# A column range for each chunk of edges in the matrix build, 196 instead of 120 of the first network's sum products inside it, and its dense layers spaced evenly

## The reference, cut to what matters

```python
src = randint(100000, 0, 3125)
dst = sort(3125 * uniform(100000) ** 2)          # sorted, dense at low numbers
h = maximum(layernorm(x), 0)
aggr = segment_sum(h[src], dst)                  # network 0
z = (1 + eps) * h + aggr
z = relu(relu(z @ W1 + b1) @ W2 + b2)
x = x + log_softmax(z)
# networks 1 to 3: again sums over the edges, dense layers, norms
```

## Time and profile before

| | us |
|---|---|
| runs | 1205.87, 1209.30, 1209.38 |
| median | 1209.3 |
| the profiled execution: its time | 1203.78 |
| its span, first to last instruction | 1202.1 |
| setup ahead of the first half | 22.7 |
| the build, halves 0 to 55 | 22.7 to 272.7 |
| rest of network 0 up to D(6) | 272.7 to 353.4 |
| the three other networks | 353.4 to 1202.1 |

### The profile page before, as it was taken

The page is one execution under the profiler, slowest core; times in us unless marked ns, Lnnn a source line. Parts: engine busy times, 40 slices in busy tenths (PEclk is TensorE's granted clock), DMA queues, the critical chain, the costliest instruction groups (busy, mean ns, idle before and its releaser), DMA issues.

```text
span 1202.1 us, 19388 instructions
## 1 busy us (share of the span) xinstructions
PE 1119.6 (93%) x6353; PEld 659.0 (55%) x6353; DVE 671.5 (56%) x1984; ACT 444.5 (37%) x1330; POOL 10.9 (1%) x36
## 2 busy tenths in 40 slices
PE   3778899999989999999898998996899999999997
PEld 3556666665554554545545545544555556544544
DVE  7999899994562235456366455365644325632211
ACT  4669988886561122211300201102421214811100
POOL 1000000000000000000000000000000000000000
PEclk9997999999989999999999998998899999999998
DMA  2100000002001013433224142399932314500001
GB/s 74 28 2 1 2 2 10 2 2 50 6 11 26 15 39 81 93 78 78 48 60 90 30 91 56 76 254 193 206 87 69 89 35 107 130 25 26 17 21 31
DMA packets 208276, 70.32 MB, mean 58 GB/s; under 512 B 180949, under 2 KB 207284, under 8 KB 208174
## 3 DMA queue, kind: packets, MB, share of 16 engines
q1 hardware_dynamic: 124702, 42.31, 16.4%
q10 hardware_dynamic: 83152, 25.52, 9.6%
q0 software_dynamic: 320, 1.22, 0.5%
HBM read 20.71 MB, written 28.26 MB: 41 GB/s over the span
## 4 chain that ended last, share of the span: by engine, by line
PE 81%; DVE 8%; DMA 4%; issue 2%; ACT 2%; ACTq 1%; DVEq 1%; SPq 0%
PE PS L1223 51%; PE PS L928 9%; PE PS L2728 4%; PE PS L917 2%; PE PS L1600 2%; PE PS L2216 2%; DMA di_d<-SM 2%; PE PS L893 2%; DVE HPb L792 2%; PE PS L2179 2%; PE PS L1718 1%; DVE HPb L789 1%; DVE HPb L737 1%; ACT ADJ L964 1%; DMA s_d<-SM 1%
## 5 line engine op out<-in xcount | busy, mean ns | idle before, releaser
L1223 PE MATMUL PS<-ADJ,HPb 125*128 125x500 bf16 (+2 forms) x2250 | 443.6, 353 | 0.0
L1223 PEld LDWEIGHTS PS<-ADJ,HPb 125*128 125x128 f16 x2250 | 219.1, 98 | 215.6 <-issue 21.9
L964 ACT CAST ADJ<-PS 126x72 f32 (+7 forms) x784 | 193.2, 315 | 44.3 <-PE PS L928 15.1
L1223 PE MATMUL PS<-ADJ,Zf 125*128 125x500 bf16 (+2 forms) x1050 | 202.1, 352 | 0.0
L928 PE MATMUL PS<-HPb 128*128 128x150 bf16 (+3 forms) x784 | 192.2, 350 | 4.3 <-ACT ADJ L964 3.1
L1223 PEld LDWEIGHTS PS<-ADJ,Zf 125*128 125x128 f16 x1050 | 102.4, 98 | 93.8 <-issue 1.3
L917 PEld LDWEIGHTS PS<-HPb 128*128 128x128 bf16 x642 | 85.2, 143 | 55.3 <-issue 31.0
L1910 DVE CUSTOM_DVE_ANT_0 HPb<-ADJ,HPb 125x625 bf16<-125x625 bf16 x125 | 101.4, 811 | 6.4 <-DMA HPb<-di_d 1.5
L917 PE MATMUL PS<-HPb 128*128 128x25 bf16 x642 | 87.4, 213 | 8.6 <-DVE HPb L792 7.1
L928 PEld LDWEIGHTS PS<-HPb 128*128 128x128 bf16 x784 | 85.6, 159 | 7.9 <-ACT ADJ L964 6.2
L2050 DVE BATCH_NORM_STATS2 WB<-PS 128x6 f32<-128x500 f32 (+2 forms) x28 | 17.6, 630 | 123.1 <-PE PS L2179 123.1
(11 more groups left out here) (363 smaller groups left out, 1112.8 us busy)
## 6 DMA issues: line engine op xcount, KB each, us to landing
adj_d<-ADJ ACTq DMA_DIRECT2D x25, 700.0 KB
HPb<-y_d SPq DMA_DIRECT2D x19, 187.5 KB, 2.8
HPb<-di_d SPq DMA_DIRECT2D x10, 250.0 KB, 3.3
adj_d<-ADJ ACTq DMA_DIRECT2D x25, 81.2 KB
ADJ<-in_x SPq DMA_DIRECT2D x1, 1562.5 KB
q_d<-HPb SPq DMA_DIRECT2D x25, 62.5 KB
HPb<-di_d SPq DMA_DIRECT2D x5, 305.2 KB
HPb<-s_d ACTq DMA_DIRECT2D x5, 250.0 KB, 3.8
```

Of the source, the lines that this page charges most:

```text
L964: e.copy(to, WPS[group % BANKS][0:PD, t0 * RESTS[q]:t1 * RESTS[q]] .rearrange("p (t d) -> p t d", t=t1 - t0)).then_inc(s_mv, 1)
L1223: mm = e.matmul(accs[q], H[0:PN, t, q, 0:P], cols, start=(t == 0 and (two or q == 0)), stop=(t == NT - 1 and (two or q == 1)), skip_group_ ...
```

## The change

Six things change:

- **A column range for each chunk.** `KEYS[k][c]` gives, for quarter k and chunk c of the group, the range of target columns that it may touch. Chunk 0 takes 0 to `HEADS[k]`, chunk 1 takes from `FROM[k]`. New checks on the input send other data to the general build; the data of this case meets them.
- **The key's order.** It is now target first, tile second (`25 * target + tile`). One table of numbers, `TAB`, serves all ranges as a slice. ACT's copies read the bank with 100 bytes from target to target (before, contiguous), and PE's joined first column is written contiguously (before, with a stride).
- **DVE writes key one-hots for chunk c of two groups together**, in all quarters, by a two-operand compare of 350+350, 350+500, 500+750 and 600+850 elements for two groups. The ring has 3 slots of two groups each.
- **PE** makes the joined first column from chunk 0 alone, and its big products have 150+150, 150+250, 225+375 and 275+425 columns.
- **196 sum products in the build:** one behind every group in halves 28 to 55. These are the ranges 0 to 2 and 46 products of range 3. 154 are left behind it, of which 54 have 500 columns.
- **Dense steps evenly spaced:** behind the build, in slots of 2 products, range c = 0 to 4 has its steps at slots 7+15c, 11+15c and 15+15c (with D(c) in the last), and `turned_z(c+1)` at 9+15c. D(5) and D(6) stay where they are in network 1's first sums. The diagonal's first part is added later, ahead of `answered(3)`.

In the setup, POOL makes one table rather than several, DVE has 8 more short comparisons for the checks, and ACT copies the keys in another layout.

```diff
-RING = 7
+RING = 3
+HEADS = (6, 6, 9, 11)
+FROM = (1, 1, 2, 4)
...
-    EARLY0, EARLY_PER = 26, 4
+    EARLY0, EARLY_PER = 28, HG
...
+    KEYS = [((0, HEADS[k] + 1), (FROM[k] if k else 0, WINS[k])) for k in range(KR)]
+    KWS = [[(c1 - c0) * NT for c0, c1 in v] for v in KEYS]
...
-                for k in range(KR):
-                    line(e.scalar_tensor_tensor(out=t3[:, k, :], in0=k3[:, k, :], scalar=float(WINS[k]), in1=t3[:, k, :],
-                                                op0=ALU.mult, op1=ALU.add))
+                line(e.scalar_tensor_tensor(out=til_f, in0=til_f, scalar=float(NT), in1=key_f, op0=ALU.mult, op1=ALU.add))
...
+                for k in range(KR):
+                    line(e.tensor_scalar(w[1][:, k:k + 1], w[3][:, k:k + 1], float(FROM[k] - 1), None, ALU.is_le))
+                    line(e.tensor_scalar(flags[:, k, 7:8], w[3][:, k:k + 1], float(HEADS[k]), None, ALU.is_gt))
...
+                def one_hots(u, c):
+                    q, g = u * 2 // QG, u * 2 % QG
+                    k0, k1 = KEYS[q][c]
+                    e.tensor_tensor(key_pair(q, u, c), TAB[:, k0 * NT:k1 * NT, :],
+                                    KTH[q][:, c, g:g + 2].rearrange("p (o g) -> p o g", o=1)
+                                    .broadcast_to([P, KWS[q][c], 2]), ALU.is_equal).then_inc(s_oh, 1)
...
-                        if q >= PAIRED:
-                            e.tensor_scalar(key_hot(q, n0 + m), IOK[q], KT[:, n0 + m:n0 + m + 1], None, ALU.is_equal)\
-                             .then_inc(s_oh, 1)
...
+                        at = h * HC + m
+                        if at % 2 == 0:
+                            unit, c = n // 2 * HG + at // (2 * GC), at // 2 % GC
+                            if unit >= RING:
+                                e.wait_ge(s_ohx, (unit - RING + 1) * 2 * GC)
...
-                        for c in range(GC):
+                        for c in range(1 if joined else GC):
...
-                            e.matmul(WPS[group % BANKS][:, 0:rests * NT], OHP[h][:, :, g * GC + c],
-                                     key_hot(q, m)[:, NTP:KWS[q]], start=(c == 0), stop=(c == GC - 1),
+                            c0, c1 = max(KEYS[q][c][0], 1), KEYS[q][c][1]
+                            e.wait_ge(s_oh, keys_told(group // 2, c))
+                            e.matmul(WPS[group % BANKS][:, (c0 - 1) * NT:(c1 - 1) * NT], OHP[h][:, :, g * GC + c],
+                                     key_hot(q, group, c, c0, c1), start=(c == 0), stop=(c == GC - 1),
...
-                        if n >= EARLY0 and g % 2 == 0:
-                            early_sum((n - EARLY0) * EARLY_PER + g // 2)
+                        if n >= EARLY0:
+                            early_sum((n - EARLY0) * EARLY_PER + g)
...
-                            e.copy(to, WPS[group % BANKS][0:PD, t0 * RESTS[q]:t1 * RESTS[q]]
-                                   .rearrange("p (t d) -> p t d", t=t1 - t0)).then_inc(s_mv, 1)
+                            e.copy(to, WPS[group % BANKS][0:PD, 0:RESTS[q] * NT]
+                                   .rearrange("p (d t) -> p t d", t=NT)[:, t0:t1, :]).then_inc(s_mv, 1)
...
-                    if c + 1 == WHOLE and not general:
+                    if c + 1 == PLAIN and not general:
                         first_diagonal()
...
-                LAG = 1 if general else WHOLE
+                FIRST, APART = 7, 15
+
+                def beside(k):
+                    if k == 2:
+                        e.wait_ge(s_mv, moved(G))
+                        turned_z(0)
+                    for c in range(NC - 2):
+                        at = FIRST + APART * c
+                        dense0(c, {at: 1, at + 4: 2, at + 8: 3}.get(k))
+                        if k == at + 2:
+                            turned_z(c + 1)
```

More of the change, by code:

```diff
@@ L77, in build @@
     STEPS = G // (2 * HG)
-    NTP = NT + NT % 2
     assert KR == len(WINS) and QG % (2 * HG) == 0
     RESTS = [w - 1 for w in WINS]
-    KWS = [NTP + r * NT for r in RESTS]
-    KWP = max(KWS)
-    PAIRED = 2
-    IOS = [w * (2 if k < PAIRED else 1) for k, w in enumerate(KWS)]
+    KEYS = [((0, HEADS[k] + 1), (FROM[k] if k else 0, WINS[k])) for k in range(KR)]
+    KWS = [[(c1 - c0) * NT for c0, c1 in v] for v in KEYS]
+    assert HEADS[0] == RESTS[0] and all(FROM[k] <= HEADS[k] + 1 <= WINS[k] for k in range(KR))
     QS = QG // (2 * HG)
@@ L101, in build @@
     HC = HG * GC
[L102 removed]
+    assert QG % 2 == 0 and HC % 2 == 0 and NCH % 2 == 0
     LAYERS = a["L2_gnn_W1"].shape[0]
@@ L149, in build @@
         RW = KR * GE
-        OHW = -(-KWP // 64) * 64
-        assert GC == 2 and RING == HG and all(w <= OHW for w in IOS)
-        IOW = sum(KWS[:3]) + P
+        OHW = -(-max(2 * sum(v) for v in KWS) // 64) * 64
+        assert GC == 2 and OHW >= NT * GW
+        TW = NT * WIN
+        IOW = TW + P
         KTW = GC * QG
+        assert RING * OHW + 2 * HC * P <= 8 * RW + 8 and NT * GW <= HC * P
         SRW = max(RW, HC * P // 2)
@@ L1459, in scaled_z @@
                     e.activation(first_of(GAT, c), first_of(ZT, c), ACT.Copy,
-                                 scale=EPS1 if c <= WHOLE and not general else EPS0).then_inc(E0["ez"], 1)
+                                 scale=EPS1 if c <= PLAIN and not general else EPS0).then_inc(E0["ez"], 1)
                 def high_parts(c):
@@ L1577, in layers @@
                         continue
-                    if c == WHOLE + 1 and not general:
+                    if c == PLAIN + 1 and not general:
                         e.wait_ge(s_adj, 2)
-                    if c >= 4:
+                    if c > 4:
                         done(E0["red"], c - 3)
@@ L1583, in layers @@
                     for t in range(start, NT):
-                        if general and c == 0:
+                        if not general:
+                            beside(slot)
+                            slot += 1
+                        elif c:
+                            dense0(c - 1, {1: 1, 5: 2, 9: 3}.get(t))
+                            if t == 2:
+                                turned_z(c)
+                        else:
                             done(E0["hp"], t + 1)
-                        if c == LAG and not general:
-                            if t == start + 2:
-                                e.wait_ge(s_mv, moved(G))
+                            if t == NT - 3:
                                 turned_z(0)
-                            dense0(0, {start + 5: 1, start + 9: 2, start + 13: 3}.get(t))
-                            if t == start + 7:
-                                turned_z(1)
-                        elif c >= LAG:
-                            dense0(c - LAG, {1: 1, 5: 2, 9: 3}.get(t))
-                            if t == 2:
-                                turned_z(c - LAG + 1)
-                        elif t == NT - 3:
-                            turned_z(0)
                         for q in range(2):
```

184 lines of the change are left out of this document (82 added, 102 removed).

## The result

The changed kernel takes 1189.05 us (median of 4 runs, 1188.01 to 1189.62), the kernel before on the same chip 1208.42 (4 runs, 1205.87 to 1209.38). That is a ratio of 0.9842, 95% interval 0.9823 to 0.9861. It is faster by 19.4 us in the medians and by 15.3 in the profiled executions (1203.78 and 1188.51). The forecast was 1196 with 1186 to 1206, its sum -13.3.

The account below looks back on a forecast made before the run. DVE was taken to bound halves 33 to 55 of the build, PE right behind, and SP's DMA loop the stage behind it. +0.5 - 12.4 - 1.4 = -13.3 us; from the median 1209.3 that gives 1196, range 1186 to 1206.

Parts of the forecast that it names:

- The sum: Whole kernel: +0.5 for setup, -12.4 for the build, -1.4 for the stage behind it, together -13.3 us.
- The build: Halves 31 to 41 go from 4.45 to 4.0 us, the last 14 from 4.79 to 4.25; together 12.4 us gained.
- register load: In the build, ACT's load of registers once a half adds some 0.3 us, an estimate.
- the added 0.1: In the build's last two quarters, 0.1 us a half added to the longest engine's time, as there is no slack anywhere.
- DVE's forms: In the build, DVE's new key compares of 600 and 850 elements cost 0.38 and 0.51 us.
- The second rival: PE becomes the bound in the build: halves of 4.6 and 4.3 us, gain 4.3 instead of 12.4, 1204 us; 17%.
- The stage behind the build: From the build's end to D(6): 79.3 us where it was 80.74, so 1.4 gained out of 16.0 us of moved products.
- the first rival: The stage behind the build shrinks in full: 16 us go instead of 1.4, 1181 us; 8%.
- D(0) to D(2): Behind the build: SP's sequence of input tiles, scales and degree rows stays at 26.07 us; PE stands still for 6.9.
- SP's loop: Behind the build: SP's DMAs from one load of degree rows to the next take 13.2, 9.1 and 10.0 us.
- DVE's cycle for a range: Behind the build, D(2) to D(6): DVE needs some 9 us a range, which fits within the distances of SP's loop.
- Setup: Ahead of the build: DVE's added subtraction, 8 short comparisons and a wait, with four key compares made one, cost +0.5 us.

Follow-up runs that it names:

- after_again: The changed kernel unaltered, run again on another chip; 1187.3 us, ratio 0.9857 to the kernel before.
- onehots_alone: The changed kernel with the old products, their order and the old dense order, so only the new key one-hots are left; ratio 0.9901 to the kernel before.
- narrower_ranges: The changed kernel with the first chunk's range cut further, HEADS (6, 5, 7, 9) for (6, 6, 9, 11); ratio 0.9888 to the kernel before.
- the six executions above: Executions with this stage's code as in the changed kernel; D(6) came 76.0, 79.2, 79.4, 79.1, 77.1 and 73.5 us behind the build.
- products_alone: The kernel before with 196 sum products in the build and the dense layers evenly spaced, but the old key one-hots; ratio 1.0074 to the kernel before.
- own_semaphore: The changed kernel with the writes of scales counting on a semaphore of their own; ratio 0.9866 to the kernel before.

## Why the prediction was right, point by point

**The sum** (-13.3, measured -15.3 in the profiled executions). It is made of +0.5, -12.4 and -1.4, and the runs gave -0.3, -11.8, -4.8 and +1.7 behind D(6). The build, which carries it, was right; that the rest comes so close is partly luck, since errors of opposite sign cancel and the stage behind the build varies by as much between executions.

**The build** (-12.4, measured -11.8). Halves 31 to 41 gave 4.6 us for the 4.9 forecast, the last quarter 6.7 for 7.5, and 0.5 came ahead of half 18, where I had none. I had put all three engines at nearly the same length and added 0.1. The runs show that the bound is ACT: 3.96 (6 x 0.507 + 0.92) and 4.27 from its own gaps, and 0.07 more on average, since in one half of four or five a gap is 0.2 to 0.3 longer. The term that was mis-sized is its register load, 0.3 in my working and 0.42 in the trace, which makes 0.12 a half, 3 us over 25 halves; the added 0.1 covered most of it. DVE's forms were right: with 0.08 of overlap taken off their mean durations, those of 600 and 850 elements are 0.385 and 0.516 us against my 0.38 and 0.51. PE's group was 0.59, not 0.567.

**What my reading of before missed.** In halves 19 to 27 of the kernel before the granted clock was 0.87 on average. In the changed kernel PE ran at half the clock, 1.2 GHz, for longer: the trace of after_again has it on record for 88 to 143 us. Its window over seven halves, then products of 250 columns from 108 to 138 us in after_again, in the changed kernel's first execution, and before (granted clock 0.83 there):

```profile
108.07:138.77 30.70, 26.42 (x148) 15.41 (x147) 24.77 (x71) 29.24 (x128) 0.00 (x0) 0.50 0.00 1
...
L924 PE MATMUL PS<-HPb 128*128 128x250 bf16 x49 | 19.7, 409 | 0.0
...
L924 PE MATMUL PS<-HPb 128*128 128x250 bf16 x48 | 19.2, 409 | 0.0
...
L928 PE MATMUL PS<-HPb 128*128 128x250 bf16 x96 | 22.6, 337 | 1.9 <-ACT ADJ L964 1.6
```

For the first execution the same window says 1.00, but that trace has no record of the clock ahead of 142 us, and the 409 ns say that it ran like after_again. Yet halves 18 to 30 took 58.15 us before and 58.14 after. So there PE has slack even at half the clock, and the 2 us that I had put in the range for it weren't needed in the build.

**The second rival**, PE as the bound, fell with onehots_alone and narrower_ranges. It was close: 4.13 us of a half of 4.27. What spoke for it was the row "PE 40.01 of 40.01". Such a row does not tell a bound: the changed kernel shows 28.02 of 28.02, and with three products of a half less the stretch is as long, with 26.56 busy. That the modelled ends fill such waits fits this, but is an inference.

**The stage behind the build** (-1.4, measured -4.8 in the profiled execution). The important call was right: of 16 us of products moved out, most became waits of PE, and the first rival's 1181 did not come. Only a part of the waits is the one that I named. For D(2) to D(6) my working has waits of 6.9, 4.2, 2.0, 3.9 and 3.4 us; the trace has 1.84, 3.98, 0.09, 1.01 and 2.20, and 5.1 more for ACT's relu, for which I had nothing. What was also off is the size of single terms. D(0) to D(2) took 24.5, not 26.07; D(4) to D(6) took 18.0, not 20.3. I had read DMA times from one execution and used them as constants, yet they differ: the same stage took 80.8 with the kernel before and 78.7 in onehots_alone, which has its order and its products. The mean over the six executions above, 77.4, is 2.4 below the mean of these two; with products_alone (74.7) it is 77.0, 2.7 below. So of the 4.8 some 2.5 belong to the moved products, nearer to the 1.4 than to the 4.8, and that with two executions on one side only.

I had also tied the stage to SP's loop alone. There is a second loop, through ACT and DVE, about as long as the first: own_semaphore took all waits for degree rows away and D(6) stayed. "DVE's cycle for a range, which needs some 9 us, fits as well" was that step: it holds where a range waits for nothing, but D(3) to D(4) takes 12 us and more in most runs, in after_again by this cycle, with DVE's addition of the first diagonal (1.46 us, L1156) in it.

**Setup** (+0.5, measured -0.3). The changed kernel began its build at 22.42 and, run again, at 22.62, before at 22.68, so there is no cost to be seen.

**The end.** 1.7 us were given back behind D(6), where nothing was changed. The six executions of unchanged code differ by 2.5 us in that stretch, so the 1.7 need no cause.

**What stays open.** Whether the moved products are worth some 2.5 us, as the stages say, or the 5 to 7 us that the ratios say (0.9901 for onehots_alone, 0.9842 and 0.9857 for both parts, measured on different chips). How much of the stage each of the two loops holds. And what makes a load of 7 registers slow.

## What to carry to other kernels

Where several engines show a full stretch, make one of them lighter and one of them heavier: an engine whose work can be cut by 3 products a half without effect is not the bound, and one on which an added 0.42 us appears in full in each half is. Count what an in-order engine's sequencer does besides its operations (register loads, register arithmetic): it stands in the same queue, hidden only while an operation runs. Before a gain is taken from a stage with DMAs in its chain, look at several executions of it: here the same code differed by more than the effect. And where a window gives a full granted clock, compare the duration of one form of matmul with that of another execution: here a 1.00 stood for a stretch without a record.

## What the hardware showed

- A load of registers on ACT costs by their number, but not evenly: 4 registers 310 ns, 8 547, 16 1007 to 1024, and 7 964. Between two copies that follow each other every 0.55 us it added 0.18, 0.42, 0.87, and 0.84 for 7, so some 0.13 of each load was hidden. In halves 18 to 30, with activations between the copies, 8, 16 and 7 added 0.17, 0.62 and 0.59: some 0.38 was hidden.
- Register operations on ACT's sequencer take 64 ns each in a row. One behind a copy is hidden in the last two quarters; seven ahead of a half cost 0.44 us.
- A copy on ACT that reads PSUM with 100 bytes between elements costs the same as one without (376 and 374 ns for 240 elements).
- The DMA of 500 scales in single elements took 14.5 us with input tiles queued ahead of it, 9.5 next, then 6.3 to 6.6. From issue to the issue of the load that waits for it, nine other executions have 13.8 to 15.1, 8.6 to 9.2 and 5.6 to 7.5.
- TensorE at a granted clock of 0.50 took 409 ns on average for a product of 250 columns, and 337 where the clock was 0.83 on average. A product of 25 columns took 227, and 186 in the changed kernel from 143 us on, at 1.00.
